# A selective scan over 16 groups: the second state of direction 0 summed on the matmul engine, and the outputs of two groups accumulated in one PSUM bank

## What is computed

```python
def step(h, inp):
    da, dbu, c = inp
    h = da * h + dbu
    return (h, jnp.einsum('bdn,bn->bd', h, c))
_, ys = jax.lax.scan(step, h0, (dA.swapaxes(0, 1), dBu.swapaxes(0, 1), Cm.swapaxes(0, 1)))
y = ys.swapaxes(0, 1) + xc * D_skip
return y * jax.nn.silu(z) @ out_w.T
```

## Time and profile before

| | us |
|---|---|
| median of 3 runs | 506.29 |
| lowest, highest | 503.71, 507.09 |
| span of the profiled execution | 503.2 |
| PE busy | 452.2 (90%) |
| DVE busy | 372.6 (74%) |
| ACT busy | 236.0 (47%) |
| POOL busy | 168.6 (34%) |

### The profile page before, as it was taken

How to read it: one execution, slowest core, us unless ns; L and a number is a source line. 1 busy time by engine, 2 the same in 40 slices (tenths; PEclk the granted TensorE clock), 3 DMA queues, 4 the chain that set the end, 5 groups by cost and what they waited for, 6 DMA issues and landing times.

```text
span 503.2 us, 6897 instructions
## 1 busy us (share of the span) xinstructions
PE 452.2 (90%) x1816; PEld 228.5 (45%) x1816; DVE 372.6 (74%) x709; ACT 236.0 (47%) x419; POOL 168.6 (34%) x164
## 2 busy tenths in 40 slices
PE   6999999999999999899967837988898888799997
PEld 3554655655554466477544501222222212275654
DVE  0257576566567668564999976899999999988756
ACT  1143323213221423355886945788887888421100
POOL 6000000100100021405450014889898989422000
PEclk9999999999999999997688977899999999999999
DMA  9992039100000000312026573366546655530000
GB/s 266 313 286 70 1 104 302 42 1 0 0 2 0 0 1 0 119 40 78 2 74 194 146 211 87 109 192 182 157 140 186 195 160 158 141 101 11 10 12 21
DMA packets 36344, 51.75 MB, mean 103 GB/s; under 512 B 5922, under 2 KB 26926, under 8 KB 36320
## 3 DMA queue, kind: packets, MB, share of 16 engines
q1 hardware_dynamic: 34736, 49.86, 33.9%
q10 hardware_dynamic: 1584, 1.59, 1.0%
HBM read 34.59 MB, written 16.52 MB: 102 GB/s over the span
## 4 chain that ended last, share of the span: by engine, by line
PE 33%; DVE 7%; SPq 6%; issue 5%; DMA 4%; ACT 3%; POOL 1%; DVEq 0%; POOLq 0%
PE ps L2072 7%; PE ps L1719 4%; PE ps L2039 4%; PE ps L1015 4%; DMA brows<-bparts 3%; PE ps L1672 3%; PE ps L1028 2%; PE ps L1685 2%; PE ps L1694 2%; SPq L1533 2%; PE ps L1060 2%; DVE da L1894 1%; PE ps L1703 1%; SPq L1007 1%; SPq L1610 1%
## 5 line engine op out<-in xcount | busy, mean ns | idle before, releaser
L1864 POOL TENSOR_TENSOR gb<-da,hb 128x512 f32<-128x512 f32 x62 | 77.8, 1277 | 61.7 <-ACT da L1784 55.2
L1784 ACT ACTIVATE da<-da 128x512 f32<-128x512 f32 x128 | 78.9, 629 | 24.8 <-DVE da L1894 20.4
L1894 DVE TENSOR_TENSOR da<-ps,expA 128x512 f32<-128x512 f32 x128 | 84.0, 686 | 7.8 <-PE ps L1672 7.1
L330 PE MATMUL ps<-area,convw 128*128 128x384 f32 (+1 forms) x220 | 73.4, 486 | 0.6 <-ACT peT L570 0.6
L397 PE MATMUL ps<-wall,peT 128*128 128x512 f32 x144 | 67.8, 593 | 0.0
L1672 PE MATMUL ps<-drows,selb 96*128 96x512 bf16 x128 | 48.5, 401 | 11.6 <-DVE da L1894 5.1
L330 PEld LDWEIGHTS ps<-area,convw 128*128 128x128 f32 (+1 forms) x220 | 41.2, 190 | 28.3 <-issue 1.4
L1685 PE MATMUL ps<-urows,brows 96*128 96x512 bf16 x96 | 35.0, 394 | 13.7 <-DVE gb L1901 7.6
L578 ACT ACTIVATE kvs<-ps 128x512 f32<-128x512 f32 x36 | 21.5, 597 | 52.6 <-PE ps L397 52.6
L570 ACT ACTIVATE peT<-ps 128x384 f32<-128x384 f32 x24 | 11.8, 491 | 66.4 <-PE ps L330 58.7
L1672 PEld LDWEIGHTS ps<-drows,selb 96*128 96x128 bf16 x128 | 11.4, 98 | 61.4 <-DVE da L1894 49.7
(11 more groups left out here) (242 smaller groups left out, 774.8 us busy)
## 6 DMA issues: line engine op xcount, KB each, us to landing
area<-in_xT SPq DMA_DIRECT2D x11, 768.0 KB
yscr<-yst SPq DMA_DIRECT2D x28, 208.0 KB
brows<-bparts SPq DMA_DIRECT2D x16, 240.0 KB, 3.0
drows<-dparts SPq DMA_DIRECT2D x14, 192.0 KB, 2.9
uparts<-pt SPq DMA_DIRECT2D x18, 128.0 KB, 2.4
dparts<-pt SPq DMA_DIRECT2D x18, 128.0 KB, 2.4
urows<-uparts SPq DMA_DIRECT2D x15, 144.0 KB, 2.9
inw<-in_in_wT SPq DMA_DIRECT2D x2, 1024.0 KB
```

Source lines behind the costliest of these rows:

```text
L330: mm = pe.matmul(bank(T_EMB + j % 2, 0, EN), convw[0:n, k, h * P:(h + 1) * P], xbuf[0:n, q, k, c * EN:(c + 1) * EN], start=(k == 0), stop= ...
L1784: act.activation(da_at(q, j), da_at(q, j), ACT.Exp, scale=-1.0).then_inc(da_ready, 1)
L1864: pool.tensor_tensor(gb_at(q, j), da_at(q, j), state, ALU.mult).then_inc({2: m2_done, 3: m3_done, 4: m4_done}[s_], 1)
L1894: dve.tensor_tensor(da_at(q, j), bank(j % 2), expA[:, j % 2, :], ALU.mult).then_inc(e_free, 1)
```

## The change

It has four parts.

1. **Second state.** Direction 0 goes the way of direction 1: b 4 gets a bank of its own (5), PE adds the product there, and ACT copies the sum. `state_2` leaves the DVE, except for the last group. A group's DVE instructions go from 13 to 12.
2. **One bank for a pair.** The output matmuls have 32 columns instead of 8: the stationary tile `cst` is widened with zeros, so that the even group's results land on rows 0 to 7 of each 32, the odd group's on rows 8 to 15 and the direct sums on rows 16 to 31, all accumulated in bank 6. ACT copies each of the two banks once in a pair, not once in a group, and `copy_direct` is gone. SP stores 2 tiles of 256 KB in a pair, where it stored 4 of 208 KB.
3. **New orders** on PE, ACT and SP.
4. **The end.** The last pair's outputs are sent in tiles of 16 rows, 4 for each k, where there were 8 for each k of 8 rows.

```diff
         def b_times_u(g, q, j):
...
-                if j < 5:
-                    pe.wait_ge(bu_used, 5 * g + j + 1)
-                    b_ = bu_bank(q, j)
+                if j < 4:
+                    need(pe, bu_used, 4 * g + j - 1)
                 else:
-                    need(pe, h2_copied, g)
-                    b_ = 4
...
-            def add_decayed(g):
-                pe.wait_ge(m2_done, 2 * g + 2)
-                pe.matmul(bank(4), ident[:, :], gb[:, 3, :], start=False, stop=True,
+            def add_decayed(g, d):
+                pe.wait_ge(m2_done, 2 * g + d + 1)
+                pe.matmul(bank(bu_bank(4 + d)), ident[:, :], gb[:, 2 + d, :], start=False, stop=True,
                           skip_group_check=True).then_inc(h2_ready, 1)
...
-                    mm = pe.matmul(ps[32 * j:32 * j + GB, (6 + k) * 512:(7 + k) * 512], cst[:, q, d, token(s_, d), :],
-                                   gb_at(q, 4 * k + j), start=True, stop=True)
+                    mm = pe.matmul(ps[32 * j:32 * j + 32, (6 + k) * 512:(7 + k) * 512], cst[:, q, d, token(s_, d), :],
+                                   gb_at(q, 4 * k + j), start=(q == 0), stop=(q == 1 and k == 1), skip_group_check=True)
...
                         spread_delta(g + 1, 1 - q, 0)
-                        add_decayed(g)
                         spread_delta(g + 1, 1 - q, 1)
-                    outputs(g, q, 0)
-                    if after:
+                        b_times_u(g + 1, 1 - q, 1)
+                        add_decayed(g, 0)
                         spread_delta(g + 1, 1 - q, 2)
-                        b_times_u(g + 1, 1 - q, 1)
+                        add_decayed(g, 1)
                         spread_delta(g + 1, 1 - q, 3)
                         b_times_u(g + 1, 1 - q, 2)
-                    if q == 1:
-                        direct(i)
-                    if after:
                         b_times_u(g + 1, 1 - q, 3)
-                    if not (first and q == 0):
-                        outputs(g - 1, 1 - q, 1)
+                    outputs(g, q, 0, i)
                     if after:
                         spread_delta(g + 1, 1 - q, 4)
                         spread_delta(g + 1, 1 - q, 5)
+                    if q == 1:
+                        direct(i)
+                    if not (first and q == 0):
+                        outputs(g - 1, 1 - q, 1, i)
...
                     if after:
                         exponential(g + 1, 1 - q, 0)
-                        copy_state(g)
                         exponential(g + 1, 1 - q, 1)
-                    copy_y(g, 0)
-                    if after:
+                        copy_state(g, 0)
                         exponential(g + 1, 1 - q, 2)
+                        copy_state(g, 1)
                     if q == 1:
-                        copy_direct(i)
+                        copy_y(i, 0)
                     if after:
                         exponential(g + 1, 1 - q, 3)
-                    if not (first and q == 0):
-                        copy_y(g - 1, 1)
+                    if q == 0 and not first:
+                        copy_y(i - 1, 1)
...
-                    if last and q == 0:
-                        send_y(sp, yst, g, 0)
-                        store_y(g - 1, 1)
-                        gather_y(0, (0, 1, 2))
+                    if q == 0 and not first:
+                        store_y(i - 1, 1)
+                    if q == 0 and last:
+                        gather_y(0)
                     elif last:
-                        send_y(sp, ylast, g, 0)
-                        gather_y(0, (3,))
                         gather_y(1)
+                        send_y(sp, 0)
```

173 lines of the change are left out of this document (80 added, 93 removed).

## The result

The changed kernel takes 527.16 us (median of 5 runs, 523.51 to 529.38), the kernel before 504.20 (503.05 to 507.09) beside it: a ratio of 1.0425, 95% interval 1.0382 to 1.0468. It is slower, by the mechanism forecast, and lies in the range of 511 to 529. The profiled execution has a span of 521.7 us against 503.2, 18.5 more. The medians lie 23.0 apart; where the 4.4 us beyond the 18.5 went, no profile shows.

What follows compares the result with a forecast made beforehand. The DVE was taken as full with PE close behind; PE's new stretch before spread 6 would set the blocks. Scan +12.5, ramp +1.1 and end +3.1 made 16.7: span 519.9, median 523 us, range 511 to 529.

Steps and rivals of the forecast that it cites:

- The mechanism: Scan blocks: PE's direct sums and outputs between spreads 5 and 6 leave the DVE idle about 0.8 and 1.8 us; +12.5.
- The rival of a covered stretch: PE's stretch before spread 6 is covered: 15.3 us a pair, 499 to 502 us in all; chance 0.07 faster, 0.08 same.
- The even block: Scan block with outputs k = 1 behind spread 5: spread 6 at 8.41 plus 0.12, 8.53 us.
- The odd block: Scan block with direct sums and outputs behind spread 5: spread 6 at 9.41 plus 0.27 and 0.18, 9.86 us.
- The surcharges: Additions to the odd block's 9.41 us: 0.27 for ACT's lateness and 0.18 for three sets of 32 columns.
- ACT's 0.27: Odd block: exponential 0 comes 0.27 us late behind the output bank's copy, and dec 0, dec 1 and b 3 with it.
- 32 columns: Wider weight loads make each set 0.06 us longer; two sets in an even block, three in an odd one.
- The ramp: First blocks: -0.5 from the shorter DVE list, 1.6 in the next block with the same clock fall; sum +1.1 us.
- The end: Behind the last spread 6: sends wait behind eight gathers, first sum at 10.6, projection about 13.8 instead of 10.66; +3.1 us.
- a send lands within 1.7 to 2.3: At the end: time in us from a send's issue to its landing, putting the first two sums at 10.3 to 10.9.
- the rival that named it: Clock falls more often, PE being idle over 3 us behind the last group: 529 us with costlier sets; chance 0.13.
- The loads gain time: Scan: loads have more time since the block is longer and SP has two stores less in a pair.

Runs made afterwards that it cites:

- e2: Changed kernel with another order on PE: b 4 and b 5 behind spread 6, outputs k = 0 ahead of b 3; 518.16 us, ratio 1.0219.
- e3: Changed kernel without the new addition of direction 0 on PE; 525.16 us, ratio 1.0378.
- e1: Changed kernel, last pair's four k = 0 gathers issued ahead of the store of the previous pair's bank k = 1; 524.15 us, ratio 1.0346.
- e12: Changed kernel with the last group's four k = 0 sends issued ahead of the four k = 1 gathers; 518.29 us, ratio 1.0196.
- e4: Kernel before with the last group's four k = 0 sends issued behind all eight gathers; 510.91 us, ratio 1.0109.
- e5: Changed kernel with another DRAM layout: four stores of 16 rows a bank, each gather 112 rows in one piece; 527.36 us, ratio 1.0437.
- e8: e7 with direction 0's second state on PE in even groups, DVE in odd; odd direct sums between spreads 2 and 3; 504.45 us, ratio 0.9976.
- e6: Kernel before with direct sums and outputs k = 1 on PE behind spreads 4 and 5; 519.51 us, ratio 1.0257.
- e7: Changed kernel with PE's order of e2, DRAM layout of e5 and the sends' order of e12; 520.14 us, ratio 1.0267.
- e9: e8 with SP's k = 0 and direct-sum stores behind the next pair's first loads, last k = 0 gathers before the k = 1 store; 499.93 us, ratio 0.9893.

## Right and wrong, step by step

- *The mechanism* was right: blocks of 8.49 and 9.36 in turn, 12 DVE instructions, PE's stretch between spreads 5 and 6, the DVE idle 0.84 and 1.60 ahead of argument 6. The rival of a covered stretch fell. e2 shows that the order did it, e3 that the addition did not. One reading was off without harm: argument 4 was put at 6.91, ahead of what 0.59 behind spread 4 (6.48) allows, and it started at 7.05; S6 is PE's in any case.
- *The even block*: 8.53 forecast, 8.49 measured.
- *The odd block*: 9.86 forecast, 9.36 measured. Its timeline holds within 0.06: b 3 at 5.20 (5.18), outputs 5.52 (5.50), spread 4 at 6.52 (6.48), direct sums 7.06 (7.00), S6 9.36 (9.41). The surcharges failed. ACT's 0.27 did not arise: four exponentials took 2.24 us, 0.52 to 0.57 apart and not 0.60, and dec 0 waited 0.21, hardly more than the 0.2 counted in any block. And 32 columns cost 0.02 a set (354.68 to 355.68 is 1.00 for 0.98), not 0.06; the second of two sets in a row started 0.89 behind the first, less than 0.98. That is the half us of the odd block, and with the even one 3.5 us in thirteen blocks.
- *The Trainium skill's rule on weight loads* ("TensorE: Matmul & The Clock Gate", section "LDWEIGHTS (loading the stationary operand)"), that speaks against wider tiles, gave 0.02 a load, and from it 0.06 or 0.16 a set were estimated. The trace agrees on the load (109 ns with 32 columns for 88 with 8), but a set is only 0.02 longer, so most of the eight stays hidden.
- *The ramp*: +1.1 forecast, -1.0 measured. I let the clock fall as it had; in the profiled run after the change it did not (1.00 for 0.83 in the second block). In the profiles of e1 to e12 the first block takes 8.6 to 10.6. This is a matter of the single execution, and should have been in the range, not in the sum.
- *The end*: +3.1 forecast, +10.5 measured; this is the term that was mis-sized. The sends' issue was right: 7.45 behind S6 (7.8). Wrong was "a send lands within 1.7 to 2.3": that came from rows in which the queue ahead was short, and the change puts eight gathers of 224 KB ahead. From the second send's issue to the first sum it was 8.6 us. So the first sum stood at 16.74 for 10.6 forecast, 6.1 of the 7.4 us; from there to the projection it was 3.85 for 3.2, and behind the projection 0.6 for nothing. Of the 10.5 us by which the first sum is later than before, e4 gives 5.9 to the place of the sends. The other 4.6 came with the layout and the larger sends; to the 7 pieces, which I had costed at nothing, e5 gives 3.2 (from the first gather on). With the sends ahead of the second gathers (e12) 4.0 are left: 1.5 because the sends are issued later (4.7 behind S6 for 3.2; the bank's copy, which now waits for the direct sums, ends at 4.4 for 3.2), and 2.5 between issue and sum, behind four gathers on 7 engines instead of three on 14.
- *The clock behind the last group* fell as in the rival that named it: PE idle 9.53 us, the clock at 0.50 from 452 to 456. It cost little behind the projection: from the projection to the end 62.96 for 62.35.
- *The loads gain time* was true for the change, but the reason it held was the long block. As soon as blocks were short (e2, e8) or the copy later (e6), the late copy held SP, and the loads behind it; in e5 and e7, with six more stores in a pair, PE waited for them up to 1.4 and 2.2 us.

The errors -3.5, -2.1 and +7.4 leave +1.8 in the span, where any one alone would have left more. That the time came so close, and into the range, is partly luck: the range had room for the first two, none for the third, and without them 7.4 more would have put the forecast at about 530, above it. The other 2.4 of the 4.2 us by which the median misses 523 is that the profiled execution lies 5.5 below the median here, where 3.1 was taken over from before.

## What to carry to other kernels

Before an instruction is taken off the fullest engine, look at what the others must do between two of its inputs: an order is good if each long piece of work stands where that engine has instructions queued, and in e9, the fastest here, each block's addition goes to the engine that has room in it. A transfer's time to landing holds only for the queue that it was measured in: count what stands ahead of it, in bytes and in engines, and put the small transfer that someone waits for first. And in a queue issued in order, a store that waits for a late copy delays every load behind it, which shows only once the blocks are short.

## What the hardware showed that I had not expected

- A gather of 7 pieces of 16 rows ran with a DMA share of 0.44 at 163 GB/s; the same 224 KB in one piece with 0.89 at 283 GB/s, and SP issued them 0.47 apart for 0.79.
- A pause of PE of 1.2 to 1.5 us inside a busy block was followed by a fall of the clock in four blocks of e6: 0.85 or 0.86 over the block, which took 11.5 to 11.8 us for 9.7; in one of them a set of outputs took 1.80 us for 1.04. Not every such pause was: e6 has odd blocks of 9.7 and 10.0 at 1.00, with pauses of 1.0 and 1.4, and e5 has five pauses of 1.2 to 1.4 without a fall. What decides between them stays open.
- In e5 packets were slow even behind the landing of the last gather (6.0 us behind its issue, at 456.8): the DMA share was 1.05 at 181 GB/s from there to 459, against 0.89 at 283 while the gathers ran. Sends from SBUF to SBUF and the gathers of direct sums run then; which of them is slow was not tried. (A packet counts in the stretch in which it starts, so the share can pass 1.)

```profile
456.80:459.00 2.20, 0.00 (x0) 0.00 (x0) 0.00 (x0) 0.00 (x0) 0.00 (x0) 0.77 1.05 181
```
